# Row maxima half an iteration ahead of the scores, chunk by chunk, in a causal attention layer

## What is computed

```python
# x: (4, 2048, 256), 16 heads of 16
Q = rope(split(layernorm(x) @ Wq.T)); K = rope(split(layernorm(x) @ Wk.T)); V = split(layernorm(x) @ Wv.T)
scores = jnp.einsum('bhqd,bhkd->bhqk', Q, K) / math.sqrt(16)
scores = jnp.where(causal_mask, -jnp.inf, scores)
attn = jax.nn.softmax(scores, axis=-1)
x = x + jnp.einsum('bhqk,bhkd->bhqd', attn, V) @ Wo.T      # heads merged
x = x + relu(layernorm(x) @ w1 + b1) @ w2 + b2
```

## Time and profile before

| what | value |
|---|---|
| median of 3 runs | 2179.07 us (2178.31 to 2179.77) |
| the profiled execution, its own time | 2177.41 us |
| its span | 2175.7 us |
| TensorE (PE) busy, matmuls | 2017.1 us, 93% |
| VectorE (DVE) busy | 1883.9 us, 87% |
| ScalarE (ACT) busy | 1448.7 us, 67% |
| GpSimd (POOL) busy | 639.2 us, 29% |
| DMA queue of SyncE | 26.0% of 16 engines |
| GpSimd busy, DMA share from 272.0 to 313.9 us | 0.00 us, 0.00 |
| granted TensorE clock, mean | 0.963 of full |

### The profile page before, as it was taken

How to read it: one execution, slowest core, us unless ns; L and a number is a source line. 1 busy time by engine, 2 the same in 40 slices (tenths; PEclk the granted TensorE clock), 3 DMA queues, 4 the chain that set the end, 5 groups by cost and what they waited for, 6 DMA issues and landing times. The chain is left out here.

```text
span 2175.7 us, 53224 instructions
## 1 busy us (share of the span) xinstructions
PE 2017.1 (93%) x19104; PEld 798.9 (37%) x19104; DVE 1883.9 (87%) x3910; ACT 1448.7 (67%) x3092; POOL 639.2 (29%) x1265
## 2 busy tenths in 40 slices
PE   5786469999999999999999999999999969999999
PEld 3443112322222222222222222222232237666776
DVE  7998899999999999999999999999996037777775
ACT  5664018888888888888888888888888942333232
POOL 7999401202212022121221212112121223333331
PEclk9999559999999999999999999999999979999999
DMA  5567303213032030330303303033020212222220
GB/s 189 205 219 208 124 10 65 53 29 75 17 71 58 24 75 17 71 57 25 76 17 71 67 16 76 16 71 71 12 66 10 77 38 83 79 93 86 84 82 25
DMA packets 126405, 152.63 MB, mean 70 GB/s; under 512 B 17248, under 2 KB 92512, under 8 KB 125920
## 3 DMA queue, kind: packets, MB, share of 16 engines
q1 hardware_dynamic: 126176, 149.67, 26.0%
HBM read 90.12 MB, written 59.24 MB: 69 GB/s over the span
## 5 line engine op out<-in xcount | busy, mean ns | idle before, releaser
L859 ACT ACTIVATE s_prob<-s_ps 128x512 f32<-128x512 f32 (+3 forms) x2560 | 1172.8, 542 | 244.1 <-PE s_ps L705 233.4
L784 DVE TENSOR_REDUCE s_part<-s_ps 128x2 f32<-128x1024 f32 x768 | 905.3, 1221 | 41.3 <-PE s_ps L689 26.0
L724 PE MATMUL s_ps<-s_prob,s_v 128*32 128x256 f32 (+3 forms) x10240 | 737.8, 360 | 14.9 <-ACT s_o L850 3.2
L705 PE MATMUL s_ps<-aq,ak 64*128 64x512 f16 (+3 forms) x2560 | 679.3, 353 | 9.0 <-DVE s_part L791 1.2
L689 PE MATMUL s_ps<-mk,mq 64*128 64x512 f16 (+3 forms) x2560 | 595.5, 360 | 59.2 <-DVE s_part L784 35.1
L889 POOL TENSOR_SCALAR_AFFINE_SELECT s_prob<-s_prob 128x128 f32<-128x128 f32 x1024 | 288.2, 295 | 1193.9 <-ACT s_prob L859 1175.2
L791 DVE CUSTOM_DVE_ANT_0 s_ps<-s_ps,mask_sb 128x512 f32<-128x512 f32 (+3 forms) x1024 | 466.1, 526 | 9.8 <-PE s_ps L689 8.1
L705 PEld LDWEIGHTS s_ps<-aq,ak 64*128 64x128 f16 x2560 | 185.3, 93 | 532.5 <-ACT s_prob L859 467.3
L724 PEld LDWEIGHTS s_ps<-s_prob,s_v 128*32 128x32 f32 x10240 | 202.0, 108 | 457.3 <-issue 332.8
L689 PEld LDWEIGHTS s_ps<-mk,mq 64*128 64x128 f16 x2560 | 143.5, 95 | 111.1 <-DVE s_part L784 67.8
L1157 ACT ACTIVATE s_h_f<-s_ps,s_b_s 128x512 f32<-128x512 f32 x128 | 88.0, 687 | 107.2 <-PE s_ps L1022 86.2
(11 more groups left out here) (86 smaller groups left out, 1535.1 us busy)
## 6 DMA issues: line engine op xcount, KB each, us to landing
v_scratch<-s_vst SPq DMA_DIRECT2D x32, 512.0 KB, 4.0
s_v<-v_scratch SPq DMA_DIRECT2D x16, 1024.0 KB, 11.6
att_scratch<-s_o SPq DMA_DIRECT2D x64, 256.0 KB, 3.1
aq<-qk_scratch SPq DMA_DIRECT2D x96, 128.0 KB, 4.2
ak<-qk_scratch SPq DMA_DIRECT2D x96, 128.0 KB, 6.8
s_xin<-x SPq DMA_DIRECT2D x16, 512.0 KB, 4.4
qk_scratch<-s_r_lo SPq DMA_DIRECT2D x64, 128.0 KB, 2.1
qk_scratch<-s_r_hi SPq DMA_DIRECT2D x64, 128.0 KB, 2.5
```

Source lines behind the costliest of these rows:

```text
L705: nc.tensor.matmul(ps[:, s_bank(s, j), q0:CH], ak[rows, p, j // 2, kb * P:(kb + 1) * P], aq[rows, p, j // 2, c * CH + q0:(c + 1) * CH], st ...
L724: last = nc.tensor.matmul(ps[32 * j:32 * j + 32, O_BANK, cols], v[:, p, kb, j, :], prob[:, s % 2, j, cols], start=kb == 0 and part == 0, s ...
L784: nc.vector.tensor_reduce(part[:, qt // 8, 2 * pair:2 * pair + 2, qt % 8, kc], ps[:, bank_of(use):bank_of(use) + 2, 0:w], AX.X, ALU.max).t ...
L859: nc.scalar.activation(prob[:, s % 2, j, q0:CH], ps[:, s_bank(s, j), q0:CH], ACT.Exp, scale=1.0 / (SQK * DK ** 0.5)).then_inc(p_done, 1)
```

## The change

Maximum step t is now counted through all iterations (t = 40 i + step), and beside the scores' step s of iteration i stands t = 40 i + s + 20 (LAG = NS // 2). So 20 steps of maxima run alone in front, and the last 20 steps of scores run alone at the end. The tiles keep the order of before (MAX_TILES is what qtile gave). The rows are made by chunk instead of by half: four row events an iteration, at maximum steps 4, 12, 24 and 40, which is beside the scores' steps 24, 32, 4 and 20. Each reduction has half the elements, and stands between the two pairs of the same step in which the transpose and the copy follow; each chunk has its own semaphore. SyncE's program is put in another order.

```diff
+LAG = NS // 2
+MAX_TILES = max_tiles()
+MAX_END = [max(m for m in range(NS) if MAX_TILES[m][0] // TPC == c) + 1 for c in range(NC)]
...
-        part = sb("s2_part", [P, 2, G, 8, NC], F32)
-        qmax = sb("s2_qmax", [P, 2, G * 8], F32)
-        nrow = sb("s2_nrow", [G * 8, 2, P], F16)
+        part = sb("s2_part", [P, NC, 2, NP, TPC, NC], F32)
+        qmax = sb("s2_qmax", [P, NC, G * TPC], F32)
+        nrow = sb("s2_nrow", [G * TPC, NC, P], F16)
...
+        def rows_after(t):
+            return [(t // NS, c) for c in range(NC) if t % NS == MAX_END[c]] if t % NS else \
+                [(t // NS - 1, c) for c in range(NC) if t > 0 and MAX_END[c] == NS]
...
         def iteration(i, p, first=False, last=False, load2=True):         
-                if load2:
-                    sp.wait_ge(m_ready, M_BEFORE + i * M_ITER)
-                    load_m(sp, ops, qk_d, i + 2, p)
-                rows(i, p, 1, second_rows_use(i, last))
                 if not first:
                     store(i - 1, NC - 1)
+                rows(i, 1)
                 if not last:
                     if not first:
                         sp.wait_ge(pv_done, NS * i + 2)
                     load_a(sp, ops, qk_d, i + 1, 1 - p)
                     load_v(i + 1, 1 - p)
+                rows(i, 2)
                 if not first:
                     load_sums(i - 1)
                 store(i, 0)
-                if not last:
-                    rows(i + 1, 1 - p, 0, rows_use(i, 0))
+                store(i, 1)
                 if not first:
                     store_rinv(i - 1)
+                if load2:
+                    sp.wait_ge(m_ready, m_use(NS * (i + 1) - 1, G - 1) + 1)
+                    load_m(sp, ops, qk_d, i + 2, p)
+                rows(i, 3)
                 if last:
...
                         load_att(sp, ops, att_d, rinv_d, 0, n, n)
-                store(i, 1)
                 store(i, 2)
+                if not last:
+                    rows(i + 1, 0)
...
                 for s in range(NS):                                       
-                    if s == HALF_STEP:
-                        pe.wait_ge(rows_in[1], 16 * G * (i + 1))
+                    t = NS * i + s + LAG
+                    if s in CHUNK_START:
+                        pe.wait_ge(rows_in[STEPS[s][0]], 16 * ROWS_DMAS * (i + 1))
...
-                        max_pair(1 - p, s, 0, m_use(i, s, 0))
+                        max_pair(t, 0)
...
+            def step(t):                                                  
+                if t < STEPS_M:
+                    max_of_pair(t, 0)
+                if t <= STEPS_M:
+                    for of, c in rows_after(t):
+                        max_of_chunk(of, c)
+                if t < STEPS_M:
+                    max_of_pair(t, 1)
+                if t <= STEPS_M:
+                    for of, c in rows_after(t):
+                        rows_out(of, c)
```

More of the change, by code:

```diff
@@ L537, in stage2 @@
         masking, selecting = sem("s2_masking"), sem("s2_selecting")
-        rows_in = [sem(f"s2_rows_in{h}") for h in range(2)]
+        rows_in = [sem(f"s2_rows_in{c}") for c in range(NC)]
         s_ready, p_done, mask_done = sem("s2_s_ready"), sem("s2_p_done"), sem("s2_mask_done")
@@ L552, in stage2, with m_use, rows_use @@
         ST = G * NS
[L554 to L571, removed]
+        STEPS_M = NIT * NS
+        def rows_after(t):
+            return [(t // NS, c) for c in range(NC) if t % NS == MAX_END[c]] if t % NS else \
+                [(t // NS - 1, c) for c in range(NC) if t > 0 and MAX_END[c] == NS]
+        rows_before = [0]
+        for t in range(STEPS_M + 1):
+            rows_before.append(rows_before[-1] + len(rows_after(t)))
+        def m_use(t, j):
+            return G * t + j + ROWS_TILES * rows_before[t]
+        def rows_use(i, c):
+            t = NS * i + MAX_END[c]
+            return G * min(t + 1, STEPS_M) + ROWS_TILES * (rows_before[t] + rows_after(t).index((i, c)))
         def bank_of(use):
@@ L585, in read_before, with crosses_diagonal @@
             return ST * i + last_in_bank + 1
[L587 to L592, removed]
+        RANK = [sum(e < MAX_END[c] for e in MAX_END) for c in range(NC)]
+        def crosses_diagonal(qt, kc):
+            return kc == qt // TPC
         block = ctx.enter_context(nc.Block())
@@ L678, in _, with max_pair @@
         def _(pe):
-            def max_pair(p, s, pair, use):
-                qt, kc = qtile(s)
+            def max_pair(t, pair):
+                p, use = t // NS % 2, m_use(t, 2 * pair)
+                if pair == 0 and t % NS == 0:
+                    pe.wait_ge(m_in[p], 128 * (t // NS // 2 + 1))
+                qt, kc = MAX_TILES[t % NS]
                 w = min(CH, (qt + 1) * P - kc * CH)
@@ L777, in _, with max_of_pair @@
         def _(dve):
-            def max_of_step(s, pair, use):
-                qt, kc = qtile(s)
+            def max_of_pair(t, pair):
+                qt, kc = MAX_TILES[t % NS]
+                use = m_use(t, 2 * pair)
                 w = min(CH, (qt + 1) * P - kc * CH)
-                if not is_diagonal(s):
+                if not crosses_diagonal(qt, kc):
                     dve.wait_ge(m_ready, use + 2)
-                    nc.vector.tensor_reduce(part[:, qt // 8, 2 * pair:2 * pair + 2, qt % 8, kc],
+                    nc.vector.tensor_reduce(part[:, qt // TPC, :, pair, qt % TPC, kc],
                                             ps[:, bank_of(use):bank_of(use) + 2, 0:w], AX.X, ALU.max).then_inc(m_read, 2)
@@ L834, in _ @@
             dve.wait_ge(part_preset, 1)
-            for s in range(NS):
-                for pair in range(NP):
-                    max_of_step(s, pair, first_use(s, 2 * pair))
-                if s == HALF_STEP:
-                    max_of_half(0, NM + G * HALF_STEP)
-                if s == ROWS1_STEP:
-                    rows_out(0, 0, G * (s + 1))
+            for t in range(LAG):
+                step(t)
             for i in range(NIT):
-                iteration(i, first=i == 0, last=i == NIT - 1)
+                for s in range(NS):
+                    step(NS * i + s + LAG)
+                    if s == RINV_STEP and i > 0:
+                        invert_sums(i - 1)
         @block.scalar
```

91 lines of the change are left out of this document (37 added, 54 removed).

## The result

The changed kernel takes 2184.13 us (median of 20 runs, 2179.24 to 2189.73) against 2179.15 us for the kernel before (20 runs, 2176.41 to 2186.34). The ratio is 1.0019, with an interval of 1.0011 to 1.0027: slower by 4 to 5 us, a small loss that the interval just keeps apart from none. The forecast was 2192. A second set of pairs gave 2183.71 against 2178.07, ratio 1.0027 [1.0017, 1.0038].

The account below looks back on a forecast made before the run. No engine has room: each step is held by the longest of TensorE, VectorE and ScalarE. Fifteen iterations at +3.25 us (48.8), +3.0 and +1.9 at the end, -41.0 in the prologue give +12.7: 2192 us, range 2164 to 2230.

Parts of the forecast that it names:

- likeliest case: Whole kernel: an iteration grows by about 3.25 us, time 2192, own range 2180 to 2215 us; chance 0.53.
- Part 1: Prologue: 20 steps of maxima alone instead of 40 ahead of the first scores; gain 41.0 us.
- Part 3: Maxima and scores 20 steps apart put narrow groups beside wide ones; cost 1.7 us an iteration, bounds 0.7 to 4.
- first rival: Mixed groups go at their bound engine's floor, streams mesh better: iteration 91.2 us, time 2155; chance 0.22 for anything faster.
- Part 4: Four row events an iteration instead of two; cost 1.4 us an iteration, bounds 0.5 and 2.4.
- Part 5: Rows DMAs wait in SyncE's strict order, chunk 1's slightly late; cost 0.2 us an iteration, up to 1.5.
- rival of late rows: Three chunks' rows each land 1 us late on SyncE's way: iteration 96.2 us, time 2234; chance 0.12.
- Part 6: Last iteration: the next stage's load starts later, so GpSimd's scaling delays its mask of step 36; cost 1.9 us.
- Part 2: End: a half iteration of scores alone instead of a whole one, 88.2 us against 85.2; cost 3.0 us.
- the head start that isn't had: Prologue: first scores wait for GpSimd or a load, all 41 us are lost, time 2233; chance 0.03.
- the pieces that cancel: Whole kernel: gains and costs cancel within 0.2%, an iteration of 92.3 to 92.85 us; chance 0.10.

Follow-up runs that it names:

- experiment 1: The changed kernel run again unaltered, for a second trace: 2183.71 us.
- experiment 2: The changed kernel with the maxima's tiles reordered so their diagonal groups stand beside the scores' diagonal groups, same 20-step lead: 2166.84 us, ratio 0.9955 to the kernel before.
- experiment 4: The changed kernel with the maxima a whole iteration (40 steps) ahead, four row events kept, SyncE's order adapted: 2214.5 us, ratio 1.0159 to the kernel before.
- experiment 5: The changed kernel with the rows of chunks 0 and 1 made together, three row events an iteration: 2171.88 us, ratio 0.9965 to the kernel before.
- experiment 6: The changed kernel with two row events an iteration, diagonal groups side by side, a lead of 24 steps: 2162.0 us, ratio 0.9916 to the kernel before.
- experiment 7: As experiment 6, with two matmuls that nobody reads added in each row event: 2151.46 us, ratio 0.9875 to the kernel before.

## Why the prediction was right or wrong

The sign was right and the time lies in the range and in the likeliest case's own range (2180 to 2215), but the loss was forecast at 12.7 us and is 4 to 5.6. Taken by the undisturbed trace of experiment 1, step by step:

| Part | forecast us | measured us |
|---|---|---|
| 1, prologue | -41.0 | -40.9 |
| 3, displaced groups, 15 x | 25.5 | 18.2 |
| 4, two more events, 15 x | 21 | 24.6 |
| 5, late rows, 15 x | 3 | 0 |
| 3 to 5 together, as read from the periods | 48.8 | 44.2 |
| 2, last iteration | 3.0 | 2.0 |
| 6, GpSimd late at the end | 1.9 | 0 |
| last stage | - | -2.4 |

(The rows of parts 3 and 4 come from the usual periods of experiments 2 and 4, 93.01 - 91.80 and 91.70 - 90.06; they add up to 42.8, and the other 1.4 of the 44.2 was not traced: it is in how the costs meet.) Attention as a whole, from the first mask to the last output copy, went from 1525.25 us to 1530.5; the forecast for it was +12.7. The span grew by 4.2, since the last stage is shorter and attention began 1.4 us later in this execution. That start differs by 1.1 us between the two traces of the kernel before, so it need not be the change's.

Of the larger misses all but part 4's lie on one side: together they make 7.4 us in the attention and 2.4 in the last stage, against a forecast loss of 12.7. The right sign therefore holds some luck, for misses of some 3 to 5 us more would have turned it.

**Part 1 held.** VectorE's first mask beside scores starts at 273.90 us, 44.5 after the first mask of all (229.36); before, the maxima alone took 85.4, from 228.5 to 313.95.

**Part 3 is the step that failed**, a term mis-sized: the phase costs 1.2 us an iteration, not 1.7, which is 7.3 us of the total. Of the missing 0.5 us, 0.15 are the sum's own: its prices, put side by side in the table of stretches, make 93.1 us, while the sum had 93.25 without its late rows. (The prediction's "2155 to 2266" for its full bounds doesn't follow from them either; they give 2159 to 2263.) The three other stretches with a displaced group came out within 0.1 us of the price; the missing 0.36 us lie in steps 4 to 15. ScalarE in order of time there:

```profile
1597.60 2.06 ACT L866 ACTIVATE s_prob<-s_ps 128x512 f32<-128x512 f32 x4 [0.36 <-PE s_ps L721]
1599.97 1.64 ACT L866 ACTIVATE s_prob<-s_ps 128x384 f32<-128x384 f32 x4 [0.30 <-PE s_ps L721]
...
1606.11 2.06 ACT L866 ACTIVATE s_prob<-s_ps 128x512 f32<-128x512 f32 x4 [1.02 <-PE s_ps L721]
```

The narrow group of the scores (steps 8 to 11) takes 1606.11 - 1597.60 = 8.51 us and not 9.2: ScalarE and TensorE run ahead of VectorE, which in the same time goes on without a gap, 22 reductions from 1590.59 in 25.65 us, 2.33 a step. So a lead won in a narrow group was not lost there, where the prediction had reasoned that the buffers are too shallow to keep one. This was its first rival's argument; it is worth 0.4 us an iteration, not the 2.3 that the rival needed.

**Part 4 held** as a mechanism and nearly in size: 0.8 us for an added event in experiment 4 and 0.70 for a removed one in experiment 5, where it had 0.7 (1.4 for two). It was the one term set too low, by some 3.6 us over fifteen iterations if experiment 4's price is taken. The idle 0.40 us before the pair behind a row copy stands in the trace at steps 4, 24 and 32, and 0.25 at step 20.

**Part 5 was too careful.** The margins were thin on paper (0 to 2 us) and were enough; the rival of late rows found nothing in any chunk. For chunk 1, the thinnest, all four rows were issued by 1584.35, and TensorE's first scores of step 4 started at 1586.77. The Trainium skill's fixed cost ("DMA: Bandwidth & Descriptors", the latency table), by which this term would have been zero, fits that no score waited; no run here shows the landing itself.

**Part 6 failed**: the load was as late as reckoned, and GpSimd's second scaling ended at 1753.41 in the second trace, 0.4 us after the first exponential that its next mask needed. But the tail was no longer for it (42.3 us). The three masks that had piled up took 0.96 us, and at the fourth GpSimd was waiting for ScalarE again:

```profile
1751.05 2.36 POOL L138 TENSOR_TENSOR o_in<-o_in,r_in 128x1024 f32<-128x1024 f32 x1 [9.31 <-DMA r_in<-rinv_scratch]
1753.37 0.96 POOL L896 TENSOR_SCALAR_AFFINE_SELECT s_prob<-s_prob 128x128 f32<-128x128 f32 x3
1754.52 0.29 POOL L896 TENSOR_SCALAR_AFFINE_SELECT s_prob<-s_prob 128x128 f32<-128x128 f32 x1 [0.20 <-ACT s_prob L866]
```

**Part 2**: the first half of the last iteration took 44.9 us and not 46.0, a part of it by the cause of part 3 (it holds the same steps 4 to 15); the half alone 42.3, as reckoned.

Neither the head start that isn't had (0.03) nor the pieces that cancel decided. The condition that was set for telling (at 92.6 us an iteration the totals are equal) was close: with the gains of parts 2 and 6 the point of no change is 90.15 + (40.9 - 2.0)/15 = 92.75, and the medians say +5.0 and +5.6 at 93.09.

## What to carry to other kernels

Shortening the lead of one software-pipelined stream over another gives a fixed gain at the two ends, and is paid each iteration by what then stands beside what: count both with rows, and after that look for an order of the work that keeps the old neighbours at the new distance. Here reordering tiles took back 1.2 us an iteration, pairing the events 1.3, and both together turned a loss of 0.2% into a gain of over 0.8%. When the total of a version with the right usual period is still too long, look at single iterations: a fall of the clock in some of them does not show in the usual period.

## What was not expected of the hardware

**The granted clock fell in iterations whose neighbours had the same work.** While both streams ran, it did so only where a row event stood in the first step of an iteration, between two diagonal groups (experiments 2, 4 and 6): 0.72 over six microseconds, 1.4 to 1.8 us lost each time, in eight iterations of experiment 6's trace and three each of experiment 2's and experiment 4's. Each of the fourteen falls begins within 3 us of that event's reduction. In the six microseconds before that event TensorE was busy for 5.80 both in the iteration whose clock fell (1556 to 1562 us) and in the one before it, whose clock did not. So its busy time there does not tell the two apart, and what picks the iterations was not found. Two matmuls of 0.3 us in that place kept it at 1.00 (experiment 7). The Trainium skill ("TensorE: Matmul & The Clock Gate", "A second HAM failure mode: psum-queue depth-cycling") tells of a clock that goes to and fro because TensorE idles for short times between groups of matmuls; experiment 7 agrees with it, where filling one such idle time took the falls away, though no run here shows why a neighbour with the same idle time was spared.

**With the scores alone the clock falls in some executions.** In the tail, where ScalarE sets the pace and TensorE is 15.5 of 16 us busy by the records, it was 0.57 for 16 us in one execution of the changed kernel (5 us lost) and 1.00 throughout in the next. The program is the same in both, and what decides it was not found. Other traces have such falls in the tail too, the longest in experiment 5's, at 0.50 from 1716 to 1736 us.

**A last stage of two lengths**, 419.5 and 422.1 us, with the same code in it. In both kernels that were traced twice the length was the same both times. It goes with the granted clock of its first 28 us, 0.63 or 0.57; why a kernel gets the one or the other is open.
